# Gated cross-attention and feed-forward kernel: the four moves of turned x spread over slots 9 and 10, and its low parts formed in slots 11 and 12

## The reference, cut to what matters

```python
# x: (16, 512, 512); ctx: (16, 512, 512); 16 heads of 32
xn = layernorm(x)
q, k, v = xn @ Wq.T + bq, ctx @ Wk.T + bk, ctx @ Wv.T + bv       # split into 16 heads
p = softmax(where(causal & mask, q @ k.T * 32**-0.5, -inf))
x1 = x + tanh(g_xattn) * ((p @ v) @ Wo.T + bo)
z = layernorm(x1); z_prev = z shifted by one token
r = sigmoid((mu_r*z + (1-mu_r)*z_prev) @ W_r.T)
k2 = square(relu((mu_k*z + (1-mu_k)*z_prev) @ W_k.T))
out = x1 + tanh(g_ffn) * r * (k2 @ W_v.T)
```

## Time and profile before

| | us |
|---|---|
| median of 3 runs | 1894.47 (1893.87 to 1899.33) |
| the profiled execution's own time | 1898.17 |
| its span on the core | 1896.4 |

### The profile page before, as it was taken

The page is one execution under the profiler, slowest core; times in us unless marked ns, Lnnn a source line. Parts: engine busy times, 40 slices in busy tenths (PEclk is TensorE's granted clock), DMA queues, the critical chain, the costliest instruction groups (busy, mean ns, idle before and its releaser), DMA issues.

```text
span 1896.4 us, 35048 instructions
## 1 busy us (share of the span) xinstructions
PE 1838.7 (97%) x10688; PEld 1426.3 (75%) x10688; DVE 1442.2 (76%) x3792; ACT 1092.5 (58%) x2055; POOL 1160.6 (61%) x1833
## 2 busy tenths in 40 slices
PE   6899999999999999999999999999899999999999
PEld 5677777777777777777777777777678888888887
DVE  6777778687777768778786877867678787887864
ACT  5655555565555556555555655656575565656552
POOL 2777677777777777776777777777753323323231
PEclk9899999999999999999999999999899999999999
DMA  7556575655656555565665566566243535354431
GB/s 221 121 121 153 132 169 128 147 141 127 155 128 168 134 139 146 130 152 129 167 138 131 148 138 153 131 157 160 85 134 104 163 99 149 111 139 126 123 100 67
DMA packets 170699, 259.06 MB, mean 137 GB/s; under 512 B 25200, under 2 KB 54896, under 8 KB 169744
## 3 DMA queue, kind: packets, MB, share of 16 engines
q1 hardware_dynamic: 161872, 241.08, 50.5%
q10 hardware_dynamic: 8640, 15.73, 4.0%
HBM read 92.06 MB, written 33.59 MB: 66 GB/s over the span
## 4 chain that ended last, share of the span: by engine, by line
PE 84%; DVE 7%; ACTq 2%; issue 2%; DMA 2%; ACT 1%; SPq 1%; POOL 0%; DVEq 0%
PE proj_ps L41 14%; PE proj_ps L42 13%; PE proj_ps L43 13%; PE score_ps L1514 9%; PE value_ps L1555 8%; PE prob_ps L1538 7%; PE score_ps L41 3%; PE score_ps L43 3%; PE score_ps L42 3%; ACTq L686 2%; PE sum_ps L1563 2%; DVE score_ps L1154 2%; PE sum_ps L43 1%; PE sum_ps L41 1%; PE sum_ps L42 1%
## 5 line engine op out<-in xcount | busy, mean ns | idle before, releaser
L1154 DVE CUSTOM_DVE_ANT_0 score_ps<-score_ps,causal 128x128 f32<-128x128 f32 (+3 forms) x1024 | 487.7, 505 | 236.7 <-PE score_ps L1514 236.4
L740 ACT ACTIVATE probs<-prob_ps 128x512 f32<-128x512 f32 (+1 forms) x768 | 395.9, 529 | 386.6 <-PE prob_ps L1538 235.6
L1514 PE MATMUL score_ps<-k_stack,q_stack 97*128 97x128 f32 (+3 forms) x1024 | 318.7, 352 | 14.5 <-DVE least L1154 13.5
L1538 PE MATMUL prob_ps<-q_stack,k_stack 100*128 100x512 f32 (+3 forms) x1024 | 283.6, 318 | 10.1 <-DMA q_stack<-max_rows 5.7
L597 POOL TENSOR_TENSOR kact<-square,kact 128x512 fp32r<-128x512 f32 x64 | 96.0, 1510 | 306.3 <-ACT kact L826 306.3
L529 POOL TENSOR_TENSOR prob_sum<-probs 128x384 f32<-128x384 f32 x256 | 262.0, 1023 | 0.0
L1514 PEld LDWEIGHTS score_ps<-k_stack,q_stack 97*128 97x128 f32 x1024 | 189.1, 190 | 89.4 <-issue 39.5
L532 POOL TENSOR_TENSOR prob_sum<-prob_sum,probs 128x256 f32<-128x256 f32 x256 | 203.4, 794 | 37.3 <-POOL prob_sum L529 0.9
L1538 PEld LDWEIGHTS prob_ps<-q_stack,k_stack 100*128 100x128 f32 x1024 | 191.8, 191 | 35.4 <-ACT probs L740 8.6
L518 POOL TENSOR_SCALAR_AFFINE_SELECT probs<-probs 128x256 f32<-128x256 f32 x256 | 111.4, 435 | 157.3 <-ACT probs L740 157.1
L522 POOL TENSOR_SCALAR_AFFINE_SELECT probs<-probs 128x256 f32<-128x256 f32 x256 | 105.2, 411 | 120.4 <-ACT probs L740 120.2
(11 more groups left out here) (185 smaller groups left out, 4711.1 us busy)
## 6 DMA issues: line engine op xcount, KB each, us to landing
k_stack<-staged SPq DMA_DIRECT2D x384, 128.0 KB
q_stack<-staged SPq DMA_DIRECT2D x384, 128.0 KB, 3.1
turning<-in_x SPq DMA_DIRECT2D x65, 256.0 KB, 4.4
res<-x SPq DMA_DIRECT2D x64, 256.0 KB, 3.5
out_x<-res SPq DMA_DIRECT2D x64, 256.0 KB, 5.4
x_io<-in_x SPq DMA_DIRECT2D x63, 256.0 KB, 5.4
x<-x_io SPq DMA_DIRECT2D x63, 256.0 KB, 3.3
xT_room_low<-turning ACTq DMA_DIRECT2D x60, 256.0 KB, 5.7
```

Source lines behind the costliest of these rows:

```text
L740: nc.scalar.activation(probs[:, u % RING, lo:hi], prob_ps[(3 * u + c) % 2][:, 0:hi - lo], ACT.Exp, scale=SCALE).then_inc(exp_done, 1)
L1154: nc.vector.tensor_tensor_reduce(out=here, in0=here, in1=causal[:, LATE - P * t:S], scale=-1.0, scalar=3e38, op0=ALU.add, op1=ALU.min, acc ...
L1514: last = nc.tensor.matmul(here[:, at:at + P * (t + 1)], q_stack[n][0:MASK_ROW + 1, j, P * t:P * t + P], k_stack[n][0:MASK_ROW + 1, j, 0:P ...
L1538: last = nc.tensor.matmul(here[:, at:at + width], k_stack[n][0:ROWS, j, P * k:P * k + P], q_stack[n][0:ROWS, j, P * k:S], start=True, stop ...
```

## The change

Two of the four moves go from slot 9 to slot 10 of ScalarE, between the exponentials, and the first two high parts to the end of slot 10. On VectorE the low parts 0 and 1 leave slot 10: part 0 goes to slot 11, where part 2 was, and parts 1, 2 and 3 stand together in slot 12, ahead of `add_output(b-1, 3)`. The low part of the attention result in slot 12 goes from before the maximum of tile 2 to behind it. No instruction is added or removed; TensorE, GpSimd and SyncE keep their orders.

```diff
@@ ScalarE, second(i, b, s)
                 if has_next and b >= 0 and s == 10:
-                    high_part_x(b + 1, 0)
+                    move_normalised(b + 1, 2)
@@ ScalarE, third(i, b, s)
-                if has_next and b >= 0 and s == 9:
-                    move_normalised(b + 1, 2)
+                if has_next and b >= 0 and s == 10:
                     move_normalised(b + 1, 3)
-                if has_next and b >= 0 and s == 10:
-                    high_part_x(b + 1, 1)
@@ ScalarE, fourth(i, b, s)
+                if has_next and b >= 0 and s == 10:
+                    high_part_x(b + 1, 0)
+                    high_part_x(b + 1, 1)
@@ VectorE, second(i, b, s)
+                if has_next and b >= 0 and s == 12:
+                    for m in range(1, T):
+                        low_part_x(b + 1, m)
                 if has_prev and s == 12:
                     add_output(b - 1, 3)
+                if b == B - 1 and s == 12:
+                    low_part_attn(K * b)
...
-                if has_next and b >= 0 and s == 12:
-                    low_part_x(b + 1, 3)
-                if now and s == 12:
-                    low_part_attn(K * b)
@@ VectorE, third(i, b, s)
-                if has_next and b >= 0 and s == 10:
+                if has_next and b >= 0 and s == 11:
                     low_part_x(b + 1, 0)
-                if has_next and b >= 0 and s == 11:
-                    low_part_x(b + 1, 2)
+                if has_next and b >= 0 and s == 12:
+                    low_part_attn(K * b)
@@ VectorE, fourth(i, b, s)
-                if has_next and b >= 0 and s == 10:
-                    low_part_x(b + 1, 1)
```

## The result

| | before | now |
|---|---|---|
| median of 9 runs each, us | 1894.84 (1893.87 to 1899.33) | 1902.72 (1900.27 to 1906.83) |
| profiled execution's own time, us | 1898.17 | 1901.27 |
| its span, us | 1896.4 | 1899.5 |

The ratio is 1.0038, with a 95% interval of 1.0027 to 1.0049. I had forecast no change, 1892.5. The time lies near the upper end of the range given, which had been drawn to take in the rival where GpSimd holds VectorE up, and at that rival's 1903.

What follows compares the result with a forecast made beforehand. TensorE bounds the kernel; its waits for VectorE leave at most a us or two per batch. Gain -14.3 plus loss 12.9 is -1.4 us: 1896.8 from the profiled 1898.17, 1893 as median, said as 1892.5; range 1882 to 1904.

Steps and rivals of the forecast that it cites:

- GpSimd holds VectorE up: Slot 12: GpSimd's context low parts delay the attention's low part; +8 to +13 us, about 1903; chance 0.22.
- Part 1: Slot 9, two moves leave: VectorE starts the low part of k3 0.63 us earlier per batch.
- Part 2: Slot 10, two low parts leave: slot 11's third score piece 0.95 us earlier, slot 9's gain included; 14.3 us.
- Part 3: Slot 10, moves behind exponentials: cost 0 on ScalarE and for SyncE's context loads, 1.2 us at the far end.
- Part 4: Slot 12, attention's low part behind the maximum: logarithm 1.2 us late, loss 0.86 us a batch, 12.9 us.
- The sign that I had set for being wrong: Slot 12: forecast wrong if VectorE's attention low part ends more than 2 us behind the second score piece.
- a wait of TensorE at q0+ for the low parts of x: Behind slot 12's third score piece: forecast wrong if TensorE's q0+ waits for VectorE's low parts; none was expected.
- The half us for the clock: 1892.5 said for 1893: shorter waits in slot 10 make low-clock stretches like batch 7's a little rarer.
- the late logarithm costs nothing: ScalarE and VectorE catch up in slots 13 to 15, so the 14.3 us gain stands alone: 1880; chance 0.08.
- uncontended: Slot 12's attention low part takes 0.74 us, gain 1.0, two clock falls don't return: 1887.5; chance 0.22.
- the moves land late: Slot 10's moves delay context loads 1.2 us and slot 12's exponentials; 0.3 us a batch, 1898; chance 0.08.

Runs made afterwards that it cites:

- GpSimd out of the way: Against the changed kernel, GpSimd's context low parts of slot 12 wait for the attention's low part; 1893.48 us, ratio 0.9980 to before.
- The last experiment: Against the changed kernel, SyncE's two context loads of slot 11 go ahead of the stack copies of k; 1905.22 us, ratio 1.0043 to before.

## Why the prediction was wrong, point by point

- **Part 1 and Part 2 (gain 0.63, 0.95 in all): right in size, wrong in the division.** 1.09 us in batch 9; o2 doesn't wait, and 0.41 us of slot 11's wait stay, where I had 0.59. Part 1 is 0.78, not 0.63: o2 begins 5.32 us behind the first move in place of 6.11. I had let the low part of k3 start behind the row that reads the maximum (818.77 + 0.14), but it starts with that row, as the low part at 818.16 does now. And the moves alone bring the third piece of slot 11 to the same 9.96 us: the low parts taken out of slot 10 added nothing, though I gave them 0.32 of the 0.95.
- **Part 3 (cost 0): right for this kernel, wrong for its reason.** The issues took 0.55 to 0.59 us. But the context loads did not come earlier with slot 11, as I had assumed (825.9 for 826.89). They go out 826.56 - 813.64 = 12.92 us behind the first move, 12.65 before, held by SyncE's own list and not by the fourth move; slot 12 came 1.1 us earlier and they did not. SyncE, slots 10 and 11 of batch 9, now, answering to the earlier trace rows:

```profile
819.21 3.32 SPq L373 DMA_DIRECT2D k_stack<-staged  x3
...
824.51 1.88 SPq L373 DMA_DIRECT2D k_stack<-staged  x3
826.56 1.95 SPq L355 DMA_DIRECT2D turning<-in_ctxT  x4
```

  and the first of these rows before:

```profile
821.03 1.84 SPq L373 DMA_DIRECT2D k_stack<-staged  x3
```

  SyncE begins the three k3 copies of slot 10 1.2 us earlier behind the first move (5.57 for 6.79) and loses 1.5 us in issuing them, 3.32 for 1.84. So it is wherever the moves stand in slot 10: in all nine such kernels these three issues take 3.3 to 3.6 us in the median of batches 1 to 14, in the three with the moves in slot 9 1.84. So the moves did make the loads late, by the length of SyncE's issues, which my Part 3 had at nothing. The logarithm's longer wait for VectorE hides this here. Where that wait is gone it costs 0.7 us of slot 12 a batch (7.62 for 6.89 with the moves alone).
- **Part 4 is the step that failed: "It takes 0.74 to 1.77 us, 0.93 in the median, and so ends near 834.2."** The start was right (0.96 behind the piece, I had 1.0), and so was the price of a late logarithm: with GpSimd out of the way it comes at 1.80, slot 13's third piece at 5.35, a loss of 0.80 where I had 0.86. The length was wrong, 1.75 in most batches. A median over the whole run was no estimate: what the length is depends on when a GpSimd instruction under way at that place ends. In this slot one is under way in thirteen of fifteen batches, and in eight it holds the low part for most of its length. The three low parts of x, in contrast, took 2.51 us where I had 2.55. A longer logarithm costs one for one: 2.80 - 1.80 = 1.0 later, 6.35 - 5.35 = 1.0 more. With holds of 0.93 to 1.06 us in eight batches (8.1 together), 0.35 to 0.72 in three (1.5) and 0.80 x 15 = 12.0 without them, Part 4 is 21.6 us. Against the 14.3 forecast as gain that is +7.3, against 1.09 x 15 = 16.4 it is +5.2; the medians differ by 7.9, the profiled spans by 3.1. The sign that I had set for being wrong, an end of the low part more than 2 us behind the score piece, came: 2.71 us. The other, a wait of TensorE at q0+ for the low parts of x, did not.
- **The half us for the clock** (1892.5 in place of 1893) had the right direction and was too small: before, the granted clock fell in slot 10 of batches 1 and 7, and those slots took 1.3 us more than the rest, 2.7 together; in the profiled execution now it falls in slot 10 of none of batches 1 to 14.
- **The rival "GpSimd holds VectorE up in slot 12"** named the mechanism, the place and the price (+8 to +13, about 1903; it came to +7.9). I gave it 0.22 against 0.40, on the ground that GpSimd might be idle or just done. It was so, or nearly so, in four batches of fifteen. The last experiment shows that GpSimd being done before it would not have helped either: with GpSimd earlier the third low part of x is held instead.

The Trainium skill has the rule for such a meeting, in "SBUF — State Buffer", section "SBUF: two separate sides": of a VectorE instruction with two SBUF inputs and a GpSimd instruction that reads SBUF, the one that starts first keeps the shared ports for the whole instruction while the other is fully blocked. The traces agree: 0.74 us with GpSimd waiting, 1.75 with it at work, and the end 0.56 us behind GpSimd's. That is 0.18 us less than the 0.74 of a free one; no run here shows why.

The other rivals: nothing of "the late logarithm costs nothing" was seen; "uncontended" held in four batches of fifteen; "the moves land late" had the context loads late, but for the landing of a move, and it was SyncE's list.

## What to carry to other kernels

When an instruction's durations in a profile spread as here, from 0.74 to 1.77 us, find out what the other engine does at the *new* place and take the length from there, not the median; and count the sum of both engines' work there, since shifting one can only move the hold. Before filling an idle gap, ask what absorbs delays there now: the 0.99 us ahead of a maximum looked spare and was what made the 1.77 us low parts free. Test an edit's parts singly: here the two moves alone win 0.6%, and the rest of the change loses 1.0% again.

## What the runs showed of the hardware that I had not expected

- VectorE's time lost to GpSimd appears in the profile as length of its own instruction (1.75 for 0.74 us), not as a wait with a releaser; the views of waits name only the innocent engine behind it. What tells it is the end: every low part that is longer than a free one, 100 of 124 before and 89 now, ends 0.54 to 0.56 us behind the end of a GpSimd instruction.
- The same DMA issue takes 0.55 to 0.59 us of ScalarE's list in slot 10, while the third and fourth move of slot 9 took 2.82 us together. SyncE was issuing for part of that time (its timeline, slot 9 of batch 9, before):

```profile
816.42 3.37 SPq L364 DMA_DIRECT2D q_stack<-staged  x3
```

  Elsewhere it does three in 1.8 to 1.9 us. But that two engines issue at once is not enough for it: now SyncE's issues cover 0.45 of the third move's 0.55 us and 0.54 of the fourth's 0.59, and neither move is slow. What these slots have in common is that the slow issues, on either engine, stand within some 3 us behind the start of a move: the third and fourth move and two of SyncE's three copies before, and two of its k3 copies now (0.95 and 1.68 us, the third 0.61). No run tests why.
